# Key rope rows and rounded queries moved by DMA, GpSimd rounding the first key tile, VectorE's remainder behind both maxima

## The reference

```python
c_q = x @ Wq_down
c_kv = x @ Wkv_down
q_c = (c_q @ Wq_up).reshape(b, s, 128, 4)
q_r = (x @ Wq_rope).reshape(b, s, 128, 64)
k_c = (c_kv @ Wk_up).reshape(b, s, 128, 4)
v_c = (c_kv @ Wv_up).reshape(b, s, 128, 4)
k_r = x @ Wk_rope                       # shared by all heads
scores = (einsum('bqhd,bkhd->bhqk', q_c, k_c) + einsum('bqhd,bkd->bhqk', q_r, k_r)) / sqrt(68)
out = einsum('bhqk,bkhd->bqhd', softmax(scores), v_c) @ Wo
```

## Time and profile before

| | |
|---|---|
| median of three executions | 2336.41 us (2326.87 to 2337.11) |
| profiled execution | 2331.98 us, span 2330.2 us |
| TensorE matmul busy | 1974.4 us, 85% |
| VectorE busy | 1630.3 us, 70% |
| ScalarE busy | 1493.7 us, 64% |
| GpSimd busy | 1456.7 us, 63% |
| DMA | 124.53 MB, 53 GB/s on average |

### The profile page before, as it was taken

How to read it: one execution, slowest core, us unless ns; L and a number is a source line. 1 busy time by engine, 2 the same in 40 slices (tenths; PEclk the granted TensorE clock), 3 DMA queues, 4 the chain that set the end, 5 groups by cost and what they waited for, 6 DMA issues and landing times.

```text
span 2330.2 us, 41105 instructions
## 1 busy us (share of the span) xinstructions
PE 1974.4 (85%) x12538; PEld 1537.0 (66%) x12538; DVE 1630.3 (70%) x1626; ACT 1493.7 (64%) x2000; POOL 1456.7 (63%) x1692
## 2 busy tenths in 40 slices
PE   8988888888888888788888888888888888887899
PEld 7766666666666666666666666666666666765666
DVE  8666777676777767677767777676767676665664
ACT  6566666766667767677666777676676766644222
POOL 5456576766667666767676776667675767523443
PEclk9999999999999999999999999999999999988899
DMA  7411111111111121111111111111111111224542
GB/s 251 140 28 41 30 47 28 35 32 37 38 35 34 25 48 28 46 29 36 32 38 38 35 35 26 46 29 47 28 35 31 38 38 37 46 71 133 162 136 68
DMA packets 145576, 124.53 MB, mean 53 GB/s; under 512 B 51518, under 2 KB 105566, under 8 KB 145502
## 3 DMA queue, kind: packets, MB, share of 16 engines
q1 hardware_dynamic: 145478, 123.87, 21.3%
q10 hardware_dynamic: 48, 0.03, 0.0%
HBM read 61.26 MB, written 35.65 MB: 42 GB/s over the span
## 4 chain that ended last, share of the span: by engine, by line
issue 24%; PE 23%; DMA 16%; SPq 13%; POOL 11%; ACT 6%; DVE 5%; POOLq 1%; ACTq 0%; DVEq 0%
PE st L1118 11%; DMA slot<-mrow 10%; SPq L784 6%; PE ob L1152 3%; SPq L739 3%; DVE mx L1027 3%; DMA w_stage<-in_Wq_rope 3%; PE sx L1133 2%; POOL k L830 2%; POOL slot L850 2%; POOL vb L886 2%; SPq L735 2%; PE ob L1084 2%; ACT pf L1000 2%; ACT pw L1008 1%
## 5 line engine op out<-in xcount | busy, mean ns | idle before, releaser
L1027 DVE TENSOR_REDUCE mx<-sx 128x4 fp32r<-128x1024 f32 x512 | 624.8, 1220 | 226.8 <-PE sx L1133 224.4
L1118 PE MATMUL st<-slot,k 128*128 128x512 f32 x1024 | 448.7, 438 | 183.1 <-DMA slot<-mrow 156.3
L1000 ACT ACTIVATE pf<-st 128x1024 f32<-128x1024 f32 x464 | 451.6, 1015 | 175.3 <-PE st L1118 173.4
L853 POOL TENSOR_TENSOR pw<-pf,pw 128x1024 f16<-128x1024 f32 x232 | 510.5, 2200 | 47.6 <-ACT pw L1008 47.6
L1052 DVE TENSOR_TENSOR pw<-pf,pw 128x1024 f16<-128x1024 f32 x232 | 398.5, 1718 | 173.4 <-ACT pw L1008 171.6
L830 POOL CAST k<-kc 64x512 fp32r<-64x512 f32 x256 | 170.1, 664 | 536.4 <-PE st L1118 536.2
L1008 ACT ACTIVATE pw<-pf 128x1024 f16<-128x1024 f32 x464 | 464.2, 1051 | 16.0 <-PE ob L1084 14.4
L1118 PE MATMUL st<-slot,krlh 128*128 128x512 f32 x1024 | 433.6, 423 | 0.0
L1133 PEld LDWEIGHTS sx<-k,slot 88*128 88x128 f32 x2048 | 317.6, 198 | 133.4 <-issue 89.7
L1133 PE MATMUL sx<-k,slot 88*128 88x256 f32 x2048 | 350.4, 295 | 51.7 <-DMA slot<-kx 34.5
L1118 PEld LDWEIGHTS st<-slot,k 128*128 128x128 f32 x1024 | 210.5, 206 | 252.1 <-issue 209.9
(11 more groups left out here) (246 smaller groups left out, 2774.2 us busy)
## 6 DMA issues: line engine op xcount, KB each, us to landing
w_stage<-in_Wq_rope SPq DMA_DIRECT2D x64, 256.0 KB, 4.6
o_scratch<-o_sb SPq DMA_DIRECT2D x256, 64.0 KB
c_scratch<-stage SPq DMA_DIRECT2D x32, 256.0 KB, 3.0
c_in<-c_scratch SPq DMA_DIRECT2D x128, 64.0 KB, 2.0
k<-kc SPq DMA_DIRECT2D x128, 48.0 KB
k<-kx SPq DMA_DIRECT2D x128, 48.0 KB
slot<-kx SPq DMA_DIRECT2D x256, 24.0 KB
slot<-kc SPq DMA_DIRECT2D x255, 24.0 KB
```

The source lines that it names most:

```text
L853: nc.gpsimd.tensor_tensor(pw[:, s, 0, 1], pf[:, 2 * (k % 2)], pw[:, s, 0, 0], ALU.subtract).then_inc(lo_done[0], 1)
L1000: nc.scalar.activation(dst, st[:, kt], ACT.Exp, scale=SCALE).then_inc(exp_done, 1)
L1027: nc.vector.tensor_reduce(mx[:, p, lo:lo + 4], sx[:, :, :].rearrange("p a (b k) -> p (a b) k", b=2), axis=AX.X, op=ALU.max).then_inc(red_d ...
L1118: last = nc.tensor.matmul(st[:, kt, h, :].rearrange("p (e n) -> p e n", e=PH), kk, q[:, s, :, h, :], start=(n == 0), stop=(n == 1))
```

## The change

Four things, all in the attention loop:

- The 64 rope rows of a step's keys and the 64 rows of rounded queries are no longer copied by GpSimd (L830, L850) but by two more DMAs on SP's queue in each body (128 KB and 256 KB). `load_content` waits for the scores of the step that used the slot before, and no longer for GpSimd.
- The stores of the attention output stand in the body with s=1, behind the copy of the queries, in place of s=2.
- ScalarE rounds only the second key tile; GpSimd rounds the first (a new 128x1024 cast from `pf` to `pw`) and then takes its remainder as before.
- VectorE's body is now: query remainders, first maximum, second maximum of the same step, content remainder (s=0), f16 remainder.

```diff
@@ load_content
-            if k > 1 or not at.first:
-                hold(sp, passed, k_ready, u + 1)
+            else:
+                hold(sp, passed, st_done, 2 * u - 6)
+            sp.dma_start(k1[0:64, s, :, :].rearrange("p a n -> p (a n)").bitcast(F32),
+                         krh[:, bp * CH:(bp + 1) * CH].bitcast(F32)).then_inc(ct_in[s], 16)
@@ sync
+            def copy_queries(at, k):
+                s = k % NS
+                hold(sp, passed, qh_done, 2 * at.step(k) + 2)
+                sp.dma_start(slot2[0:64, s].rearrange("p e a n -> p (e a n)").bitcast(F32),
+                             slot1[0:64, s].rearrange("p e a n -> p (e a n)").bitcast(F32)).then_inc(s2_in[s], 16)
@@ body of sync
+                if at.live(k - 1) and k <= STEPS:
+                    copy_queries(at, k - 1)
...
-                elif k % NS == 2 and at.live(k - 7):
-                    store_o(at, k - 7)
+                elif k % NS == 1 and at.live(k - 6):
+                    store_o(at, k - 6)
@@ body of gpsimd
-                    if at.live(k - NS):
-                        hold(pool, passed, st_done, 2 * u - 6)
-                    nc.gpsimd.tensor_copy(k1[0:64, s, :, :].rearrange("p a n -> p (a n)"),
-                                          krh[:, bp * CH:(bp + 1) * CH]).then_inc(k_ready, 1)
...
-                if at.live(k - 1) and k <= STEPS:
-                    hold(pool, passed, qh_done, 2 * u)
-                    nc.gpsimd.tensor_copy(slot2[0:64, (k - 1) % NS], slot1[0:64, (k - 1) % NS]).then_inc(s2_done, 1)
                 if at.live(k - 4) and at.split(k - 4):
-                    hold(pool, passed, hi_done, 2 * at.parts(k - 4) - 1)
+                    hold(pool, passed, exp_done, 2 * u - 7)
+                    hold(pool, passed, av_done, u - 7)
+                    nc.gpsimd.tensor_copy(pw[:, s, 0, 0], pf[:, 2 * (k % 2)]).then_inc(hi_done[0], 1)
+                    hold(pool, passed, hi_done[0], at.parts(k - 4))
@@ rounded, scalar
-                for kt in range(2):
-                    act.wait_ge(exp_done, 2 * v + kt + 1)
-                    nc.scalar.activation(pw[:, k % NS, kt, 0], pf[:, 2 * (k % 2) + kt], ACT.Copy).then_inc(hi_done, 1)
+                act.wait_ge(exp_done, 2 * v + 2)
+                nc.scalar.activation(pw[:, k % NS, 1, 0], pf[:, 2 * (k % 2) + 1], ACT.Copy).then_inc(hi_done[1], 1)
@@ body of vector
-                if at.live(k - 2) and k - 2 < STEPS:
-                    maxima(at, k - 2, 1)
...
-                    if k % NS:
-                        maxima(at, k - 1, 0)
...
-                        maxima(at, k - 1, 0)
+                    for half in range(2):
+                        maxima(at, k - 1, half)
@@ scores, row_scores
-                    pe.wait_ge(s2_done, v + 1)
+                    pe.wait_ge(s2_in[s], 16 * (at.turn(k) + 1))
...
-                    pe.wait_ge(ct_in[s], 48 * (at.turn(k) + 1))
+                    pe.wait_ge(ct_in[s], 64 * (at.turn(k) + 1))
```

More of the change, by code:

```diff
@@ L79, in __init__ @@
         self.o_stored = sem("o_stored")
-        self.k_ready = sem("k_ready")
         self.ql_done = sem("ql_done")
@@ L665, in attention @@
         ql_done = at_sems.ql_done
-        s2_done = sem("s2_done")
-        k_ready = at_sems.k_ready
+        s2_in = [sem(f"s2_in{s}") for s in range(NS)]
         ct_in = at_sems.ct_in
@@ L676, in attention @@
         exp_done = sem("exp_done")
-        hi_done = sem("hi_done")
+        hi_done = [sem(f"hi_done{kt}") for kt in range(2)]
         lo_done = [sem(f"lo_done{kt}") for kt in range(2)]
@@ L725, in load_content @@
         def load_content(sp, at, k, heads=PH):
-            s, u = k % NS, at.step(k)
+            s, u, bp = k % NS, at.step(k), (k // NS) % NBP
             c = content[(k // NS) % 2]
@@ L826, in body @@
                 if at.live(k) and k < STEPS:
-                    bp = k // NS
-                    if at.live(k - NS):
-                        hold(pool, passed, st_done, 2 * u - 6)
-                    nc.gpsimd.tensor_copy(k1[0:64, s, :, :].rearrange("p a n -> p (a n)"),
-                                          krh[:, bp * CH:(bp + 1) * CH]).then_inc(k_ready, 1)
                     if at.first and k < 2:
-                        pool.wait_ge(k_ready, k + 1)
                         pads(k + 2)
@@ L837, in body @@
                     if s == 2 and at.live(k + 2):
-                        hold(pool, passed, k_ready, u + 1)
+                        if at.live(k - NS):
+                            hold(pool, passed, st_done, 2 * u - 6)
+                        if at.live(k - 5):
+                            if at.split(k - 5):
+                                hold(pool, passed, lo_done[0], at.parts(k - 5))
+                            else:
+                                hold(pool, passed, vx_ready, u - 4)
+                        if k == 14 and not at.last:
+                            hold(pool, passed, w_ready, NS * at.g + NS + 1)
                         copies(k // NS + 1, at.turn(k) + 1)
@@ L1050, in body @@
                 if at.live(k - 4) and at.split(k - 4):
-                    dve.wait_ge(hi_done, 2 * at.parts(k - 4))
+                    dve.wait_ge(hi_done[1], at.parts(k - 4))
                     nc.vector.tensor_tensor(pw[:, k % NS, 1, 1], pf[:, 2 * (k % 2) + 1], pw[:, k % NS, 1, 0],
@@ L1127, in row_scores @@
                     pe.wait_ge(qh_done, 2 * v + 2)
-                    pe.wait_ge(ct_in[s], 48 * (at.turn(k) + 1))
-                    if at.first and k < 2:
-                        pe.wait_ge(k_ready, k + 1)
+                    pe.wait_ge(ct_in[s], 64 * (at.turn(k) + 1))
                 for h in range(2):
@@ L1427, in sync_tail @@
             for landed in at_sems.ct_in:
-                sp.wait_ge(landed, 48 * NT)
+                sp.wait_ge(landed, 64 * NT)
             for row in (0, 32):
@@ L1432, in sync_tail @@
             sp.wait_ge(at_sems.mrow_in[1], 16 * NT)
-            sp.wait_ge(at_sems.k_ready, NS * NT)
             sp.wait_ge(at_sems.o_stored, 64 * (NT - 2))
@@ L1489, in pool_tail @@
     def pool_tail(pool, k):
-        if k == 1:
+        if k == 0:
             pool.wait_ge(at_sems.w_ready, NS * G2)
@@ L1499, in pool_tail @@
             nc.gpsimd.memset(a2[:, :, :, :], 0.0).then_inc(ab2_zero, 1)
-        if k == 9:
+        if k == 10:
             nc.gpsimd.memset(b2_raw, 0.0).then_inc(ab2_zero, 1)
@@ L1555, in act_tail @@
                 act.wait_ge(b2_loaded, 16 * 4)
-                act.wait_ge(at_sems.k_ready, NS * NT)
+                for landed in at_sems.ct_in:
+                    act.wait_ge(landed, 64 * NT)
                 nc.scalar.activation(hh[:, 0, :], b2_raw, ACT.Copy, scale=0.5).then_inc(b2_hi, 1)
```

## The result

| | median | ratio to before |
|---|---|---|
| before | 2334.35 us | |
| after | 2249.68 us (2243.86 to 2256.88) | 0.9644 [0.9605, 0.9683] |

The account below looks back on a forecast made before the run. It took TensorE to wait 3.3 us per 32.0 us turn for the row of maxima, delayed by GpSimd through SP's stores. 27.85 + 1.05 + 0.3 = 29.2 us per turn gave 2170 us (2090 to 2240); stated range 2030 to 2270.

Parts of the forecast that it names:

- A: Rival: VectorE's chain is shorter or partly hidden, a turn runs at TensorE's pace of 26, about 1970 us; chance 0.20.
- C: Rival: no change, row of maxima or s=2 content late again behind copies and stores, about 2336 us; chance 0.07.
- part one: SP no longer waits for GpSimd: the 3.3 us wait per turn goes; 0.3 us booked for late s=2 content.
- The row of maxima: SP's DMA lands 2.1 us after issue; TensorE's 3.3 us wait per turn goes, 4.9 us with its slow matmuls.
- The content of s=2: Content DMAs on SP behind the stores, the tight place: 0.3 us per turn booked (0 to 1.5).
- The Trainium skill's rule: Stores use two DMA engines, new copies sixteen; by it the content wait is about 1 us, time 40 us longer.
- Part three: GpSimd's new 128x1024 cast takes 1.04 us; its cast and remainder end 5.8 us after the body's scores start.
- Part four: VectorE's chain between successive sx1 takes 6.0 us, longer than TensorE's plain bodies; gain partly given back, turn 27.85 us.
- Part five: VectorE and GpSimd remainders meeting: mostly pass each other, together 1.05 us per turn (0 to 7.6).
- The sum: 27.85 + 1.05 + 0.3 = 29.2 us per turn against 32.0, 2.8 less.
- B: Rival: GpSimd's remainder meets VectorE's in every body, 1.9 us four times a turn, 2540 us, milder 2380; chance 0.11.

Follow-up runs that it names:

- wide: The changed kernel with each of the four output stores taking both column halves of 32 partitions instead of one half of 64: 2090.28 us, 0.8939.
- pool_queries: The changed kernel (narrow stores) with the rounded queries copied by GpSimd again instead of by the 256 KB DMA: 2166.23 us, 0.9261.
- wide_act_rounds: The wide kernel with ScalarE rounding both key tiles again and GpSimd only splitting: 2071.71 us, 0.8873.
- wide_late_pool: The wide kernel with VectorE's old order, and GpSimd's rounding and remainder held back until the body's projections: 2143.94 us, 0.9175.
- before_vector: The kernel before with VectorE's new order alone: 2259.72 us, 0.9668.
- wide_act_content: The wide kernel with ScalarE rounding both key tiles again and VectorE's content remainder between the two maxima of s=0: 2039.02 us, 0.8707.
- wide_content_early: The wide kernel with VectorE's content remainder between the two maxima of s=0 instead of behind both: 2070.29 us, 0.8856.

## Why the prediction was right, and where its size was off

Direction and range held; the forecast was 80 us too fast. 2250 lies 10 us outside the forecast's own bounds of 2090 to 2240, and inside the stated range by the part that rivals A and C lent it. Two of its signs failed as well: sx0 still waits for a DMA, which it had named as the sign of being wrong in part one, and the clock is 0.951 and not near full. That the miss is only 80 us is partly luck, as the sum below shows. By its steps:

- **The row of maxima** (part one): right. Its wait is gone, and SP is free ahead of it. It lands in 2.6 us, not 2.1.
- **The content of s=2** (part one): the step that failed. I booked 0.3 us, 0 to 1.5. The schedule held: from the start of body s=1 at 1018.86 the stores went at +6.3 (forecast 5.9) and sx0 of s=3 was ready at 1034.1, +15.3 (forecast 15.5). What failed was the 7.95 us for which stores hold up what follows, taken from the kernel before: here the content landed 1035.84 - 1025.18 = 10.7 us after the first store's issue, at +17.0 and not +14. That is 1.87 us of wait and then work at half clock. Wide against after puts the term at 2.6 us per turn; 2.3 us too little over 63 turns is 145 us. The 7.95 was read from a single 8 KB row right behind the stores. The content rows are four DMAs, the last issued 5.5 us after the first store, and they have the 256 KB copy ahead of them. The fall of 84 us without that copy (pool_queries) shows that it takes part, though not how: there, too, content landed late, just before 757.12 for stores that began at 747.41, 9.7 us after the first. So the copy explains about 1 us of the 2.7 beyond 7.95, and it starts the stores about 0.7 us later; how the rest divides is open.
- **The Trainium skill's rule**: from "DMA: Bandwidth & Descriptors" (the section on why a DMA increments its semaphore by 16), by which the slowest dimension sets how many engines a DMA uses, I had worked out that this wait would be the likely one, because the stores would use two engines and the copies sixteen. The trace of after agrees with two engines (a share of 0.10 and 0.11 where 2/16 is 0.125), and wide, which changes only the shape of the stores, agrees with the cause. My estimate of its price, 1 us, was below the measured 2.6. The forecast with it would have been 2210, nearer to 2250 than my 2170.
- **Part three**: the new cast takes 1.04 us, as taken. That it is free on the path was not so by 19 us (wide_act_rounds, on the kernel with wide stores), through GpSimd and not through ScalarE.
- **Part four**: from sx1 to sx1, s=3 to s=0 1048.75 - 1040.17 = 8.58 (forecast 8.6); s=1 to s=2 1030.70 - 1024.32 = 6.38 (6.0, the rest is the 1.71 us remainder at 1026.24); s=0 to s=1 6.64 (7.25). The last was over-booked, since 1.25 for the content remainder was itself a meeting with GpSimd, whose remainder ran from 1022.67 to 1024.82 in that turn; alone it takes 0.69. Of the waits, 0.80 in s=1 (1.3 forecast) and 0.90 at the values (0.9) stand where they were forecast; the 0.55 in s=2 is more than the 0.05 to 0.2 that a chain of 6.0 leaves there. (A slip that changes nothing: the four bodies of TensorE in the prediction add up to 25.3 us and not 25.4.)
- **Part four's worth** was missed. I called the new order a gain partly given back; it is also what spares the transposes their wait and keeps VectorE mostly out of GpSimd's way. Undoing it costs 30 us here and 73 us with wide stores.
- **Part five**: 1.05 us per turn forecast. The mean of 1407 ns against 1.23 alone is 0.7 on four f16 remainders.
- **The sum** without the drain was 28.9 us per turn; wide shows 28.1. The two errors partly cancel: 2.3 too little for the content, about 0.8 too much for VectorE, leaves the 1.5 by which 30.7 exceeds 29.2.
- **Rivals.** C is what happened, in the content only and at about half its price (30.7 - 29.2 = 1.5 of its 2.8). B's mechanism is real, but belongs to the old order. A is not reached even in the fastest kernel, whose turn is 27.3 us.

Open: how much of wide's gain is SP's shorter issue; how the two old-order costs (meetings, place of the maxima) divide, since wide_late_pool moved the wait to the values; and why part four alone takes so much of the wait for the row of maxima away in before_vector. The trace shows a wait of up to 3.6 us for VectorE in its place, which fits a wait hidden behind another one, but no run separates that.

## What to carry to other kernels

When a DMA lands late behind others on its queue, look at the shape of those ahead and not only at their bytes: the same 64 KB written with a slowest dimension of 32 in place of 2 gave 160 us in the changed kernel, 110 in the kernel before, and 18 in the changed kernel without its large copy. So undo each of two suspects alone and both together, since either can look like the whole cause. A delay read from one small transfer behind a slow one (7.95 us) was too short for several larger ones (10.7). And where two engines share work of equal size, ask at what moment each starts it: VectorE's order, with the same instructions, was worth 30 us with narrow stores and 73 with wide ones.

## What the runs showed of the hardware that I had not expected

- Four 64 KB stores of slowest dimension 2 move 27 to 45 GB/s where they alone drain (pool_queries, 1014 to 1016), at a DMA share of 0.12 to 0.14, and content rows behind them landed 10.7 us after the first one's issue in the turn shown. With slowest dimension 32 each store lands in 2.3 us (wide).
- The same copy of 256 KB within SBUF is worth a gain of 57 us or a loss of 84 us by what drains beside it.
- VectorE's small remainder (64x512) takes 0.69 us alone (after). It takes 1.25 where it starts 0.7 us before the end of GpSimd's remainder (before, and much the same in wide_act_content), and 2.31 where it starts 0.4 us behind that remainder's start (wide_content_early, mean 2.15). Each time it ends 0.55 us after GpSimd's. The large one (128x1024) takes 1.23 alone and 2.6 to 3.2 in a meeting.
